# The stages ahead of the first tile of a two-layer graph kernel, laid out anew

## What is computed

```
# layer 0, for each block of 64 nodes
Wh = x @ W;  e = leaky(Wh @ a, 0.2)
S = softmax(adj_block * e[..., None]);  out = S @ Wh
y = leaky(out @ W1 + b1, 0.01);  y = leaky(y @ W2 + b2, 0.01);  z = y @ W3 + b3 + out
x1 = layernorm(x + layernorm(z) * g + b)
# layer 1, heads h = 0..3 of 32 columns
hh = x1 @ W_proj.T
score[i,j,h] = leaky(s_left[i,h] + s_right[j,h] + adj[i,j] * we, 0.2)   # -9e15 where adj <= 1e-5
out = layernorm(x1 + leaky(x1 + softmax_j(score) @ hh + bias, 0.5))
```

## Time and profile before

| | us |
|---|---|
| median of 3 runs | 2027.68 (2026.42 to 2027.81) |
| the profiled execution | 2030.75, of which the span is 2028.7 |
| first X of POOL starts, in the span | 116.12 |
| from there to the end of the span | 1912.6 |

### The profile page before, as it was taken

One profiled execution on the slowest core, in us unless ns is written; L12 is line 12 of the kernel. 1 busy time (PEld: TensorE's weight loads), 2 busy tenths in 40 slices (PEclk: granted clock), 3 DMA queues, 4 the chain that ended last, 5 costly groups with the idle time before them and its releaser, 6 DMA issues.

```text
span 2028.7 us, 34544 instructions
## 1 busy us (share of the span) xinstructions
PE 1833.7 (90%) x11304; PEld 913.2 (45%) x11304; DVE 1855.1 (91%) x3529; ACT 1563.7 (77%) x3448; POOL 1858.8 (92%) x664
## 2 busy tenths in 40 slices
PE   5779999999999999999999999999989999888885
PEld 4644444445444544444444444445445444433332
DVE  1259998999989999999999999899998999999997
ACT  6657887888878878779877888788877887766664
POOL 2069999999999999999999999999999999999996
PEclk7779999999999999999999999999999999999999
DMA  3122333333233342424323323332322333243220
GB/s 98 64 70 83 105 109 100 97 97 110 88 106 97 95 114 68 121 94 115 99 82 123 94 88 105 97 118 84 110 83 97 118 89 97 73 123 99 92 65 11
DMA packets 138618, 191.69 MB, mean 94 GB/s; under 512 B 22344, under 2 KB 56520, under 8 KB 138440
## 3 DMA queue, kind: packets, MB, share of 16 engines
q1 hardware_dynamic: 138440, 189.49, 31.4%
HBM read 180.82 MB, written 8.65 MB: 93 GB/s over the span
## 4 chain that ended last, share of the span: by engine, by line
DVE 41%; PE 23%; issue 19%; POOL 13%; ACT 3%; SPq 1%; DVEq 0%; DMA 0%; ACTq 0%; POOLq 0%
DVE X L1012 28%; PE psum L1108 19%; POOL X L471 12%; DVE X L1002 5%; PE psum L1265 4%; DVE x1s L900 1%; DVE st L873 1%; POOL haug L456 1%; DVE est L873 1%; DVE res L960 1%; DVE lky L966 1%; DVE psum L951 1%; ACT o_sb L628 1%; DVE mv L879 0%; PE psum L1184 0%
## 5 line engine op out<-in xcount | busy, mean ns | idle before, releaser
L471 POOL TENSOR_TENSOR X<-RHO,E 128x1536 f32<-128x1536 f32 (+1 forms) x512 | 1776.2, 3502 | 75.5 <-ACT E L727 71.4
L1012 DVE SCALAR_TENSOR_TENSOR X<-psum,s_j,X 128x512 f32<-128x512 f32 x2048 | 1399.2, 741 | 51.3 <-POOL X L471 46.3
L1108 PE MATMUL psum<-X,haug 128*33 128x512 f32 x4096 | 991.9, 605 | 3.1 <-DVE X L1012 3.1
L727 ACT ACTIVATE E<-psum,we_s 128x512 f32<-128x512 f32 x512 | 397.1, 776 | 254.3 <-PE psum L1108 253.0
L1265 PEld LDWEIGHTS psum<-ident,adj_sb 128*128 128x128 f32 x2048 | 288.4, 141 | 577.7 <-DVE X L1012 412.4
L1265 PE MATMUL psum<-ident,adj_sb 128*128 128x128 f32 x2048 | 434.9, 293 | 112.0 <-DVE X L1012 105.6
L1108 PEld LDWEIGHTS psum<-X,haug 128*33 128x33 f32 x4096 | 196.1, 111 | 428.8 <-issue 392.4
L732 ACT ACTIVATE psum<-psum,we_s 128x512 f32<-128x512 f32 x512 | 381.2, 745 | 0.0
L1108 PE MATMUL psum<-sgn_ident,pen 128*128 128x128 bf16 x2048 | 378.4, 220 | 0.0
L690 ACT ACTIVATE pen<-adj_sb,pen_bias 128x512 bf16<-128x512 f32 x512 | 367.0, 717 | 0.4
L1002 DVE TENSOR_TENSOR X<-psum,E 128x512 f32<-128x512 f32 x496 | 334.7, 675 | 2.9 <-ACT psum L534 2.9
(11 more groups left out here) (220 smaller groups left out, 1511.1 us busy)
## 6 DMA issues: line engine op xcount, KB each, us to landing
adj_sb<-in_adj_dram SPq DMA_DIRECT2D x128, 1024.0 KB, 5.1
RHO<-rho_scratch SPq DMA_DIRECT2D x32, 1024.0 KB, 9.8
out_dram<-o_sb SPq DMA_DIRECT2D x32, 256.0 KB, 2.9
xg<-in_x_dram SPq DMA_DIRECT2D x28, 256.0 KB, 5.6
blk<-in_adj_dram SPq DMA_DIRECT2D x56, 64.0 KB, 5.3
X<-in_x_dram SPq DMA_DIRECT2D x2, 256.0 KB, 3.2
W_sb<-in_L_gnn_W_dram SPq DMA_DIRECT2D x4, 64.0 KB, 2.1
X<-in_adj_dram SPq DMA_DIRECT2D x4, 64.0 KB, 3.4
```

Source lines behind the costliest of these rows:

```text
L471: Q.tensor_tensor(X[m % NX][:, 0:heads, :], RHO[:, g % 2, 0:heads, :], bc(E[m % NE][:], 1, [P, heads, GROUP]), ALU.mult).then_inc(B_pool, 1)
L727: A.activation(E[m % NE][:], TA[m % NT], ACT.Exp, scale=we_s[:, 3:4], bias=we_s[:, 5:6]).then_inc(E_sb, 1)
L1012: ins = V.scalar_tensor_tensor(slot[:, h, :], TA[m % NT], s[:, k, h:h + 1], slot[:, h, :], ALU.mult, ALU.max)
L1108: return T.matmul(o, l, r, start=start, stop=stop)
```

## The change

All of it but three small edits lies ahead of tile 0.

- Logits and the softmax's scaling of groups 0 to 5 go from ACT (four instructions a group) to DVE (`first_logits`, `first_soft`, one instruction with two inputs in SBUF). The norm of x1 for groups 0 to 3 goes from ACT to DVE (`first_norm`); `r_shift` on POOL falls away there.
- For groups 0 to 3 z is computed once. DVE multiplies it by rstd and g (`first_zn`), and POOL adds xb (`first_residual`); `chain_zg` runs from group 4 on.
- The chains of groups 0 to 3 are interleaved in their later stages, the chain of group 4 is spread among them, and that of group 5 partly. One mask is made before the norms instead of four. The weights of layer 1 are prepared later (`wp_in`), the loads are reordered, and PE starts on `const_set` 3 instead of after all memsets.
- rho of the first group is broadcast by PE (`first_rho`: four matmuls a head, with a column of `ident` broadcast as the stationary operand) and copied to RHO by ACT; the fourth head stays in the bank RB. The store to DRAM remains for the later groups.
- E and G of tiles 0 to 2 are made among the preparation.
- In every body: hsum is four matmuls on `x1sum`, which ACT accumulates in `chain_x1T` (one more instruction each, to read the sum), in place of 16 matmuls on `hb`.
- zg of group 4, its `z_rstd` apart, stands in the host work of tiles -32 to -1, which PE now runs inside tile 0, and DVE behind its tile 0.

```diff
             def load_rho(g):
...
+                if g > 2:
+                    sp.wait_ge(RB_ps, g - 2)
...
+            def first_residual(c):
+                pool.wait_ge(zn_first, c + 1)
+                pool.wait_ge(xb_sb, c + 1)
+                Q.tensor_tensor(x1_of(c)[:], x1_of(c)[:], xb[set_of(c)], ALU.add).then_inc(r_first, 1)
...
             def tile(m):
                 g, k = divmod(m, JT)
-                if k == 0:
-                    pool.wait_ge(rho_in, 16 * (g + 1))
+                if m < 2:
+                    pool.wait_ge(rho_first, HP + m)
+                if k == 0 and g > 0:
+                    pool.wait_ge(rho_in, 16 * g)
...
+            def first_rho(h):
+                act.wait_ge(rhoB_ps, h + 1)
+                copy(RHO[:, 0, h, :], rho_bank(h)).then_inc(rho_first, 1)
...
+            def first_logits(c):
+                s = set_of(c)
+                dve.wait_ge(wh_sb[1], c + 1)
+                V.tensor_tensor(blk[s], blk[s], bc(e_l[s][:], 2, [P, GT, K]), ALU.mult).then_inc(exb_first, 1)
...
+            def first_zn(c):
...
+                for t in range(GT):
+                    ins = V.scalar_tensor_tensor(x1_of(c)[:, t, :], mid_bank(c)[:, tsl(t)], rstd[s][:, t:t + 1], g_bc[:],
+                                                 ALU.mult, ALU.mult)
...
+            def first_norm(c):
...
+                    ins = V.tensor_scalar(x1_of(c)[:, t, :], x1_of(c)[:, t, :], mv[s][:, t, 0:1], rstd[s][:, t:t + 1],
+                                          ALU.subtract, ALU.mult)
...
             for m in range(MT):
                 tile(m)
+                if m == 0:
+                    chain_rin(NB + 1)
+                    first_soft(NB + 1)
+                    for i in range(-BODY // 2, 1):
+                        for part in range(3):
+                            host(i, part)
...
+            def first_rho(h):
+
+                pe.wait_ge(rho_sb, 1)
+                for t in range(GT):
+                    row = ident[0:H * JT, h * JT + t:h * JT + t + 1].broadcast_to([H * JT, P])
+                    ins = mm(rho_bank(h)[:, tsl(t)], row, rho_T[:])
+                ins.then_inc(rhoB_ps, 1)
...
-            def make_hsum(nb, j):
+            def make_hsum(nb):
+                if nb == 0:
+                    pe.wait_ge(rho_first, 3)
                 pe.wait_ge(rho_sb, nb + 1)
-                for t in range(CHUNK * j, CHUNK * (j + 1)):
-                    ins = mm(BK_A[:, 0:1], hb[:, t, 0:D], tiny[:], start=(t == 0), stop=(t == JT - 1))
-                if j == NC_ - 1:
-                    ins.then_inc(hsum_ps, 1)
+                pe.wait_ge(x1T_sb, NB * (nb + 1))
+                for u in U:
+                    ins = mm(BK_A[:, 0:1], WpT[:, 0:D], x1sum[:, u:u + 1], start=(u == 0), stop=(u == NB - 1))
+                ins.then_inc(hsum_ps, 1)
...
+            for h in range(H):
+                first_rho(h)
+            transposes(1)
+            chain_y2(NB)
+            transposes(2)
+            for j in range(2):
+                chain_z(NB, j)
+            make_hsum(0)
             pe.wait_ge(back_in, 16 * H)
 
             for m in range(MT):
...
                 if m + NT < MT:
                     transposes(m + NT)
+                if m == 0:
+                    for i in range(-BODY // 2, 0):
+                        host(i)
                 host(m)
```

More of the change, by code:

```diff
@@ L640, in chain_x1T @@
                     act.wait_ge(h_ps[1], c)
-                copy(x1T_of(c), tail_bank(c)).then_inc(x1T_sb, 1)
+                if c % NB == 0 and c > 0:
+                    act.wait_ge(hsum_ps, c // NB)
+                A.activation(x1T_of(c), tail_bank(c), ACT.Copy,
+                             accum_out=x1sum[:, c % NB:c % NB + 1]).then_inc(x1T_sb, 1)
             def chain_h(c, j):
@@ L678, in make_hcol @@
                     at = 64 * (h % 2)
-                    ins = copy(hcol[nb % 2][at:at + DH, h // 2:h // 2 + 1], BK_A[h * DH:(h + 1) * DH, 0:1])
+                    ins = copy(hcol[nb % 2][at:at + DH, h // 2:h // 2 + 1], BK_A[h * DH:(h + 1) * DH, 0:1], TINY)
                 ins.then_inc(hcol_sb, 1)
@@ L727, in tile, with make_G @@
                 A.activation(E[m % NE][:], TA[m % NT], ACT.Exp, scale=we_s[:, 3:4], bias=we_s[:, 5:6]).then_inc(E_sb, 1)
-                if k == 1:
+            def make_G(m):
+                A.activation(TA[m % NT], TA[m % NT], ACT.Exp, scale=we_s[:, 2:3], bias=we_s[:, 4:5]).then_inc(G_ps, 1)
+            def tile(m):
+                g, k = divmod(m, JT)
+                if m >= NT:
+                    make_E(m)
+                if k == 1 and g > 0:
                     copy_RB(g)
@@ L789, in _ @@
             copy(W_sb[:, D:D + 1], TA[1][:, 0:1]).then_inc(prep_act, 1)
-            for r in range(2):
-                copy(back[r][:], ident[:]).then_inc(prep_act, 1)
             for c in U:
@@ L808, in _ @@
-            for c in U:
-                chain_ST(c)
+            chain_xT(NB)
+            chain_exp(0)
+            chain_exp(1)
+            chain_exp(2)
+            chain_ST(0)
+            chain_exp(3)
+            for c in (1, 2, 3):
+                chain_ST(c)
+            chain_wh(NB, 0)
+            act.wait_ge(prep_pe, 3)
+            A.activation(b1p[:], RB[:, HR:HR + 1], ACT.Identity, scale=-1.0, bias=b1_sb[:]).then_inc(prep_act, 1)
             for c in U:
                 chain_oT(c)
+            chain_wh(NB, 1)
@@ L812, in _ @@
+            for r in range(2):
+                copy(back[r][:], ident[:]).then_inc(prep_act, 1)
             for c in U:
                 chain_y1(c)
+            chain_exp(NB)
             for c in U:
                 chain_y2(c)
+            act.wait_ge(prep_dve, N_PREP)
+            penalty(0)
             for c in U:
                 chain_ssq(c)
-            act.wait_ge(prep_dve, N_PREP)
-            for m in range(LEAD):
-                penalty(m)
-            for c in U:
                 z_rstd(c)
-            for c in (NB, NB + 1):
-                chain_xT(c)
@@ new lines, in _ @@
+            act.wait_ge(prep_pe, 5)
+            copy(WpT[:, 0:D], RB[:, 0:D]).then_inc(prep_act, 1)
+            copy(WpT[:, D:HR], RB[:, D:HR]).then_inc(prep_act, 1)
+            chain_xT(NB + 1)
+            first_rstd(1)
+            chain_ST(NB)
+            chain_x1T(0)
+            chain_wh(NB + 1, 0)
+            first_rstd(2)
+            chain_x1T(1)
+            chain_h(0, 0)
+            first_rstd(3)
+            chain_oT(NB)
+            chain_x1T(2)
+            chain_h(1, 0)
+            chain_h(0, 1)
@@ L1041, in host @@
                         (make_raw, make_lam)[part](nb)
+            first_logits(0)
+            first_logits(1)
+            chain_max(0)
+            first_logits(2)
+            chain_max(1)
+            first_logits(3)
+            chain_max(2)
+            chain_max(3)
+            for c in U:
+                chain_rin(c)
+                first_soft(c)
             dve.wait_ge(wb_in, 16 * N_WB)
@@ L1363, in _ @@
                     chain_z(c, j)
-            for c in U:
-                for j in range(2):
-                    chain_zg(c, j)
-            for c in (NB, NB + 1):
-                chain_xT(c)
-            for j in range(2):
-                for c in (NB, NB + 1):
-                    chain_wh(c, j)
-            for c in U:
-                chain_x1T(c)
-            for j in range(2):
-                for c in U:
-                    chain_h(c, j)
+            pe.wait_ge(const_set, N_CONST)
+            pe.wait_ge(zn_first, 1)
+            transposes(0)
+            pe.wait_ge(wp_in, 16 * N_WP)
+            pe.wait_ge(prep_act, 3)
+            T.transpose(RB[:, 0:D], Wp_sb[:], ident[:]).then_inc(prep_pe, 1)
+            mm(RB[:, D:HR], Wp_sb[:], wlr[:]).then_inc(prep_pe, 1)
+            chain_xT(NB + 1)
+            chain_ST(NB)
+            chain_x1T(0)
+            chain_wh(NB + 1, 0)
+            chain_x1T(1)
+            chain_h(0, 0)
+            chain_oT(NB)
+            chain_x1T(2)
+            chain_h(1, 0)
+            chain_h(0, 1)
+            chain_wh(NB + 1, 1)
+            chain_x1T(3)
+            chain_h(2, 0)
+            chain_h(1, 1)
+            chain_h(3, 0)
+            chain_h(2, 1)
+            chain_h(3, 1)
+            chain_y1(NB)
             make_rmT(0)
```

289 lines of the change are left out of this document (166 added, 123 removed).

## The result

| | before | after |
|---|---|---|
| median | 2027.05 us (4 runs, 2024.05 to 2027.81) | 1991.7 us (4 runs, 1991.44 to 1992.15) |
| the profiled execution, its span | 2030.75, 2028.7 | 1992.15, 1990.3 |
| first X of POOL | 116.12 | 76.09 |

The ratio is 0.983, with an interval of 0.9815 to 0.9844: the change is worth 35.4 us. The forecast was 1986.1 with its own range of 1981 to 1992, and a range of 1977 to 1999 in all; 1991.7 lies just inside the upper end of the narrower one.

The account below looks back on a forecast made before the run. Three engines are full in the loop, so the serial path to POOL's first X was taken to decide: 116.1 - 73.5 - 1.5 + 0.5 = 41.6 us off 2027.7 gives 1986.1 us, own range 1981 to 1992, overall 1977 to 1999.

Parts of the forecast that it names:

- when does the first X start: Whole kernel: time is the start of POOL's first X, 116.12 before, plus 1912.6 us of loop.
- from the last wh copy to oT: Softmax ahead of the first tile: from 16.5 to the start of oT of group 0 at 27.0, 10.5 us.
- from the last hb to the first X: Factors, haug and rho's broadcast behind the projection: 9.5 us, from 64 to a first X at 73.5.
- The walk: Step-by-step sum along the new order: first X at 73.5, loop start losing 1.5, bodies gaining 0.5; 41.6 us gained.
- Nothing up to the last wh copy moves: Opening: the copy waits for group 3's loads, issued in the same order, and ends at 16.5.
- Between oT and z: MLP and z of the first four groups: 19.2 us, z ending at 46.2; a later clock rise 2 more.
- VectorE's work on the norms: Ahead of the projection: DVE starts at 42.5, works 12.5, waits 0.7 and 1.3; last x1 ready at 57.0.
- the projection: Behind the norms, overlapping them: last hb 7 us after the last x1, at 64, out of 61.5 to 67.
- A low clock in all gaps: Rival, softmax to loop start: clock rises late, first X at 81; gain 28, 2000 us; chance 0.22.
- The higher clock nearly throughout: Rival, from 40 us on: denser PE keeps the higher clock, first X at 68.5; 1980 us; chance 0.20.
- loss in the loop: Rival case about the loop losing time; chance 0.03.
- no change: Rival case that the tiles don't start earlier, which would need an overlooked wait; chance 0.01.

Follow-up runs that it names:

- filler in all gaps: Changed kernel with idle transposes of the identity in all of TensorE's gaps of the first 70 us; 1982.83 us.
- late start: Changed kernel, but TensorE again begins only when all of POOL's constants are set, at 6.3 us instead of 3.4; 1992.17 us.
- the second of the last two kernels: Changed kernel with idle transposes in TensorE's gaps, POOL's additions and VectorE's work on groups 4 and 5 later, and group 0's norm on ACT; 1978.65 us.
- the first of them: Changed kernel with idle transposes in TensorE's gaps of the first 70 us, POOL's additions and VectorE's work on groups 4 and 5 later; 1979.82 us.

## Why the prediction was right, and where it was off

**Right.** The reading that the kernel is "when does the first X start" held: the loop came out 1.6 us longer in all, where 1.0 was forecast. The three parts that were undone were each on the path: one z, VectorE in place of ACT for the scaling, and rho by TensorE cost 6.5, 4.2 and 3.9 when undone alone; the norm of group 0, undone, cost nothing. The largest part was not undone in any run. That three tiles' transposes, the sums and the chain of group 4 no longer stand between haug and tile 0 shows only in the trace, as 21.0 of the 40.0 us. Two stretches came out within about 0.2 us, from the last wh copy to oT, and from the last hb to the first X. For the second, the clock at the broadcast was taken from the same place of the kernel before, and it was 0.50 again.

**Off: 5.6 us too fast.** The walk promised 41.6; the profiled executions differ by 2030.75 - 1992.15 = 38.6, so the walk is short of 3.0. "Nothing up to the last wh copy moves" looked at the loads and not at TensorE's rate: the wh matmuls ran at half rate (0.86 us a pair from 12.31 to 15.75, 0.45 behind), and the copy ended 1.7 later. In the eight other runs with this opening it ended 1.3 to 3.0 later than forecast, so the new order has a part in it and not chance alone; how large a part isn't shown. Between oT and z the clock rose only after 4 us (1.1). And VectorE's work on the norms was under-sized (1.2): it took 15.6 us from 45.23 and not 14.5, with 1.08 for a norm and not 0.92, and 1.4 of waits for ACT and not 0.7; that POOL's addition holds it up once, by 1.0, was in the sum. Against that the projection overlapped more than I had it (1.1 less), and the two stretches above were 0.3 shorter together. The loop adds 0.6, and 0.2 comes back outside the span.

Another 3.3 is the base. I took the walk's sum off a median of 2027.7, but made it on an execution of 2030.75, whose clock was 0.972 where others of that kernel had 0.973 to 0.978; over the medians the gain is 35.4. It may be that part of what the change removed was there only in that execution, but no trace of a faster one was read, so this is not shown. The shift of the median from 2027.68 to 2027.05 goes the other way, by 0.6.

One reading was wrong without harm. The 239.4 and 239.0 for the first and the third body are the widths of stretches laid down by hand. From the first X of one body to that of the next it is 241.0 for the first (116.12 to 357.14), 239.1 for the second and 238.7 for the third, so before, too, the loop lost some 2 us at its start. The sum didn't use it; the reading that the loop runs at its pace from its first tile did.

**The rivals.** "A low clock in all gaps" named the cause of two of the three steps that came out longer, but put it too high: 28 of gain. The third, VectorE's norms, is not the clock's. "The higher clock nearly throughout" was 1980 at a first X of 68.5; made to happen, it gave 1982.8 and 68.2. Beside POOL VectorE's instructions lasted longer in three places, by 0.9, 1 and 2 us (1.30 for 0.42, 2.05 for 1.08, 2.38 for 0.42), and at least the first was on the path. The stretches of the first and the third body read a granted clock of 0.98 and 0.99, so "loss in the loop", to which the forecast gave 0.03, didn't show, and neither did "no change".

## What to carry to other kernels

Starting an engine earlier needn't help: TensorE began at 3.4 us instead of 6.3 here, and its first wh pairs took 0.86 us instead of 0.45. Look at the gaps that the new order leaves on TensorE, and price the work behind each gap at the longer of the times that the trace shows for it (here about twice the shorter), or fill the gap. Removing the wait at the top of the list may only move it: ask what the new order makes late. Before a small difference is put down to an edit, look for a run without the edit that shows it too. And a sum made on one profiled execution belongs to that execution; if it lies above its median, part of the gain may be there alone.

## What the runs showed of the hardware

In the opening the durations tell TensorE's rate, and the column of the granted clock doesn't. In the changed kernel the column reads 1.00 in every stretch from 0 to 22 us, and yet a wh pair took 0.86 us from 12.31 to 15.75, as it did at 0.50 later (the pair at 54.88 in the run with the norm of group 0 on ACT), and 0.45 from 15.75 on. Its trace holds no record of the clock before 15.7 us. Four runs show the same, here with the time of a step in us and the place where it starts:

| run | first record of the clock | ahead of it | behind it |
|---|---|---|---|
| changed kernel | 15.7, 1.00 | four transposes 1.12 at 11.40; a pair 0.86 from 12.31 | a pair 0.45 from 15.75; four transposes 0.60 at 17.54 |
| kernel before | 12.2, 1.00 | four transposes 1.12 at 9.90 | a pair 0.45 from 12.26 |
| filler in all gaps | 10.6, 1.00 | four transposes 1.12 at 8.45 | four transposes 0.66 at 12.32; a pair 0.45 from 12.82 |
| late start | 18.0, 1.00 | four transposes 1.11 at 12.43; a pair 0.86 from 13.34 | a pair 0.45 from 18.28 |

In all four the column reads 1.00 both ahead of that record and behind it.

At the broadcast of rho, with 15 transposes (2.2 us) put into waits of 0.70, 0.98 and 0.45 us, the clock read 1.00 from 66 to 74, where the changed kernel without them has 0.59 at 70 to 72 and 0.50 at 72 to 74, and the first X came 2.5 us earlier. Ahead of the first x1, with the same 26 transposes there (3.0 us), the clock held at 1.00 in the run with filler in all gaps and in the second of the last two kernels; in the first of them it fell to 0.50 at 52 to 54.

A load of 1 MB that repeats the same rows of DRAM on all 128 partitions (RHO) took 9.7 us from issue to landing in the median, and one of 1 MB of adj 5.2, in the run with rho through DRAM.
